# A first feed-forward product of ternary numbers, with its rank part as a product of its own

## What is computed

```python
def _bitlinear(x, w_latent):
    scale = jnp.clip(jnp.mean(jnp.abs(w_latent), axis=1, keepdims=True), 1e-05, None)
    tern = jnp.clip(jnp.round(w_latent / scale), -1.0, 1.0)
    w = w_latent + (tern - w_latent)
    return x @ (w * scale).T
h = _bitlinear(x, w_fc) + gate * (x @ v.T @ fast_b.T @ u.T)     # 256 -> 1024, rank 16
r = jnp.maximum(h, 0.0)
x = layernorm(x + _bitlinear(r * r, w_proj))                    # 1024 -> 256
```

## Time and profile before

| | |
|---|---|
| median of 3 runs | 2974.2 us (2971.97 to 2974.21) |
| the profiled execution | 2975.85 us |
| its span | 2974.1 us |
| mean granted clock of TensorE | 0.989 |
| busy, TensorE / VectorE / ScalarE / GpSimd | 97% / 80% / 73% / 64% |
| DMA | 57.54 MB, 19 GB/s over the span |

### The profile page before, as it was taken

One profiled execution on the slowest core, in us unless ns is written; L12 is line 12 of the kernel. 1 busy time (PEld: TensorE's weight loads), 2 busy tenths in 40 slices (PEclk: granted clock), 3 DMA queues, 4 the chain that ended last, 5 costly groups with the idle time before them and its releaser, 6 DMA issues.

```text
span 2974.1 us, 60896 instructions
## 1 busy us (share of the span) xinstructions
PE 2875.0 (97%) x20655; PEld 2306.4 (78%) x20655; DVE 2368.3 (80%) x6879; ACT 2164.4 (73%) x5699; POOL 1892.6 (64%) x2484
## 2 busy tenths in 40 slices
PE   7999999999999999999999995999999999999996
PEld 5677777777777777777777774778888888888885
DVE  6878978888888888798798787777777777777775
ACT  5766766776776776676676673677888888888884
POOL 5866866766776776676676684245555555555455
PEclk9999999999999999999999998999999999999998
DMA  2000000000000000000000003000000000000000
GB/s 73 22 9 16 23 9 16 23 9 16 23 8 16 23 8 16 23 9 16 23 9 16 23 29 100 8 8 8 22 19 19 15 15 15 15 15 15 8 15 22
DMA packets 51234, 57.54 MB, mean 19 GB/s; under 512 B 3024, under 2 KB 48608, under 8 KB 50928
## 3 DMA queue, kind: packets, MB, share of 16 engines
q1 hardware_dynamic: 49776, 51.94, 5.4%
q10 hardware_dynamic: 1152, 1.70, 0.2%
HBM read 36.86 MB, written 16.78 MB: 18 GB/s over the span
## 4 chain that ended last, share of the span: by engine, by line
PE 78%; ACT 9%; DVE 5%; issue 4%; POOL 3%; ACTq 0%; DVEq 0%; POOLq 0%
PE pj L299 17%; PE qk L364 9%; PE sc L335 9%; PE v_up L1321 7%; PE qk L379 6%; PE tp L354 5%; PE k L1321 4%; PE sc L354 4%; PE out L1412 3%; PE q L1321 3%; PE down L1412 3%; PE qk L310 3%; ACT b_y L96 2%; PE qk L317 2%; ACT b_ring L1504 2%
## 5 line engine op out<-in xcount | busy, mean ns | idle before, releaser
L719 POOL TENSOR_SCALAR a_ex<-a_ex,a_rc 128x384 f32<-128x384 f32 (+1 forms) x1024 | 535.1, 533 | 376.8 <-DVE a_rc L601 376.8
L488 ACT ACTIVATE a_ex<-a_ex,a_nm 128x384 f32<-128x384 f32 (+1 forms) x1024 | 575.3, 565 | 37.0 <-DVE a_nm L594 27.7
L594 DVE CUSTOM_DVE_ANT_0 a_ex<-sc,a_mask,a_rn 128x384 f32<-128x384 f32 (+1 forms) x1024 | 531.7, 543 | 8.7 <-PE sc L335 8.6
L1853 POOL TENSOR_TENSOR b_alo<-b_ring,b_ahi 128x512 fp32r<-128x512 f32 x128 | 169.4, 1324 | 415.8 <-DVE b_ring L1676 377.1
L494 ACT ACTIVATE a_pt<-tp 128x256 f32<-128x256 f32 (+1 forms) x512 | 222.7, 435 | 289.9 <-PE tp L354 289.9
L703 POOL TENSOR_TENSOR a_qr<-a_ra,a_rb 128x256 f32<-128x256 f32 x512 | 370.1, 734 | 89.7 <-DVE a_rb L576 89.7
L335 PE MATMUL sc<-a_kT,a_qT 64*64 64x256 f32 (+1 forms) x4096 | 307.6, 415 | 0.9 <-DVE a_nm L594 0.9
L364 PE MATMUL qk<-a_pt,a_v 128*64 128x384 f32 (+1 forms) x2048 | 303.9, 439 | 0.6 <-DVE a_pt L606 0.6
L606 DVE COPY a_pt<-sc 128x384 f32<-128x384 f32 (+1 forms) x400 | 203.7, 509 | 91.5 <-PE sc L354 86.2
L364 PEld LDWEIGHTS qk<-a_pt,a_v 128*64 128x64 f32 x2048 | 136.0, 136 | 142.5 <-issue 122.3
L575 DVE TENSOR_TENSOR a_ra<-pj,s_a_rot 128x256 f32<-128x256 f32 x512 | 212.8, 416 | 33.8 <-ACT s_a_sq L473 31.3
(11 more groups left out here) (279 smaller groups left out, 9166.0 us busy)
## 6 DMA issues: line engine op xcount, KB each, us to landing
s_res<-x SPq DMA_DIRECT2D x16, 512.0 KB, 3.9
y<-s_res SPq DMA_DIRECT2D x16, 512.0 KB, 2.9
s_y<-y SPq DMA_DIRECT2D x16, 512.0 KB, 3.9
a_xin<-x SPq DMA_DIRECT2D x15, 512.0 KB, 5.0
out<-b_y SPq DMA_DIRECT2D x15, 512.0 KB, 2.9
a_xin<-wqkv SPq DMA_DIRECT2D x8, 256.0 KB, 3.0
a_raw<-wqkv SPq DMA_DIRECT2D x3, 384.0 KB, 8.5
a_raw<-wqkv ACTq DMA_DIRECT2D x3, 384.0 KB, 12.0
```

The costliest lines, as they stand in the source:

```text
L488: e.activation(ex[h][w][:, 0:width], ex[h][w][:, 0:width], ACT.Exp, bias=nm[:, w, h:h + 1], scale=-1.0, accum_out=rs[:, w, h:h + 1]).then_ ...
L594: e.tensor_tensor_reduce(out=ex[h][w][:, 0:width], in0=SC[w % 2][h][:, 0:width], in1=mem['mask'][:, off:off + width], scale=rn[:, par, 4 * ...
L719: e.tensor_scalar(row, row, 0.0, rc[:, w, h:h + 1], ALU.add, ALU.mult).then_inc(g['exn_pool'], 1)
```

## The change

The up product is now made of the bare ternary numbers, which need no low part; scale and rank part are handled elsewhere.

- `mem['f_t']` holds the transposed ternary numbers. `pe_up` multiplies them with y3hi and y3lo, four products, and adds a fifth: `u_st` times `xv`.
- `xv` is v times the rows: `pe_rank_rows`, new, four products into the bank k, once for each sequence at c = 0. Then `dve_rank_rows`, new, reads that bank twice. The 128 rows of contraction are four strips of 32, in each of which 16 rank rows lie: strip 0 holds the rounded result (the subtraction takes nothing off there), strip 1 its low part, strip 2 the product with v's low part, strip 3 again the first. `u_st` has the rounded gate · fast_b · u / scale in strips 0 to 2 and its low part in strip 3.
- The scale of each output is applied on reading: `act_relu` gets `scale=st[:, 4, c:c + 1]`, `dve_square` multiplies by the same column in place of the maximum with 0.
- At c = 0, `pe_down` is called before `pe_up`.
- Preparation: the difference, the sum, the scaling, `pe_fc_rank`, `dve_fc_rank`, `act_fc_high`, `dve_fc_low` and `dve_rank` are gone. `dve_rank_up` and `dve_rank_down` come in at (-1, 3) and (-1, 4), and `pe_rank` gets eight transposes that spread 1 / scale over all partitions. The loads of w_proj wait for the ternary numbers (`tern_dve`) and no more for the sum.

```diff
     def pe_rank(e):
         for k in range(2):
-            e.matmul(O[k][0:RANK, :], mem['fb'], mem['u_t'][:, k * 512:(k + 1) * 512], start=True,
+            e.matmul(O[k][:, :], mem['fb'], mem['u_t'][:, k * 512:(k + 1) * 512], start=True,
                 stop=True).then_inc(w['bu_pe'], 1)
...
+        for k in range(2):
+            for t in range(4):
+                last = e.transpose(D[k][:, t * P:(t + 1) * P],
+                    st[:, 5, 4 * k + t:4 * k + t + 1].to_broadcast([P, P]), ident[:, :])
+            last.then_inc(w['inv_pe'], 1)
...
+    def dve_rank_up(e):
+        for k in range(2):
...
+            e.tensor_copy(raw[:, k * 512:(k + 1) * 512], O[k][:, :]).then_inc(w['u_dve'], 1)
...
+            e.scalar_tensor_tensor(raw[:, k * 512:(k + 1) * 512], raw[:, k * 512:(k + 1) * 512],
+                mem['gate'][:, 0:1],
+                D[k][:, :], ALU.mult, ALU.mult).then_inc(w['u_dve'], 1)
...
+        e.tensor_copy(mem['u_st'][:, :], raw).then_inc(w['rank_dve'], 1)
...
+        e.tensor_tensor(low, raw[3 * RANK_STEP:P, :], low.bitcast(F32), ALU.subtract).then_inc(w['rank_dve'], 1)
...
+    def pe_rank_rows(e, s):
+        e.wait_ge(g['y3l_dve'], 2 * s + 2)
...
+        if inside(s + 2):
+            e.wait_ge(g['ku_dve'], HC * (s + 3))
+        else:
+            e.wait_ge(g['sq_dve'], FC * s)
+        parts = [(c, x) for c in range(DC) for x in y3_split(s)]
+        for k, (c, x) in enumerate(parts):
+            last = e.matmul(K_BANK[:, :], mem['v_st'][:, c, :], x[:, c, :], start=k == 0, stop=k == len(parts) - 1)
+        last.then_inc(g['xv_pe'], 1)
...
     def pe_up(e, s, c):
...
-        pe_split_product(e, up_bank(s, c), mem['fhi'], mem['flo'], *y3_split(s), c).then_inc(g['h_pe'], 1)
+        bank, parts = (up_bank(s, c), [(k, x) for k in range(DC) for x in y3_split(s)])
+        for n, (k, x) in enumerate(parts):
+            e.matmul(bank[:, :], mem['f_t'][:, k, c * P:(c + 1) * P], x[:, k, :], start=n == 0, stop=False)
+        if c == 0:
+            e.wait_ge(g['xk_dve'], s + 1)
+        e.matmul(bank[:, :], mem['u_st'][:, c * P:(c + 1) * P], mem['xv'][:, :], start=False,
+            stop=True).then_inc(g['h_pe'], 1)
...
+        if c == 0 and inside(b - 2):
+            pe_rank_rows(e, b - 2)
         if c == 0 and inside(b + 1):
             pe_y2(e, b + 1, 1)
+        if c == 0 and inside(down[0]):
+            pe_down(e, *down)
         if inside(b - 2):
             pe_up(e, b - 2, c)
...
-        if inside(down[0]):
+        if c and inside(down[0]):
             pe_down(e, *down)
...
-        e.activation(mem['r'], up_bank(s, c)[:, :], ACT.Relu).then_inc(g['r_act'], 1)
+        e.activation(mem['r'], up_bank(s, c)[:, :], ACT.Relu, scale=st[:, 4, c:c + 1]).then_inc(g['r_act'], 1)
...
+    def dve_rank_rows(e, s):
+        e.wait_ge(g['xv_pe'], s + 1)
+        e.tensor_scalar(mem['xv'][:, :], K_BANK[:, :], mem['low_rows'][:, 0:1], None,
+            ALU.mult).then_inc(g['xs_dve'],
+            1)
+        e.wait_ge(g['xs_dve'], s + 1)
+        e.tensor_tensor(mem['xv'][:, :], K_BANK[:, :], mem['xv'][:, :].bitcast(F32),
+            ALU.subtract).then_inc(g['xk_dve'],
+            1)
...
-        e.scalar_tensor_tensor(mem['sq'][c % 2], up_bank(s, c)[:, :], 0.0, mem['r'], ALU.max,
-            ALU.mult).then_inc(g['sq_dve'], 1)
+        e.scalar_tensor_tensor(mem['sq'][c % 2], up_bank(s, c)[:, :], st[:, 4, c:c + 1], mem['r'],
+            ALU.mult, ALU.mult).then_inc(g['sq_dve'], 1)
```

More of the change, by code:

```diff
@@ L1063, in dve_biases, with dve_scales @@
         e.wait_ge(w['ready_dve'], 2)
[L1065 to L1068, removed]
+    def dve_scales(e, count, n, scale):
+        link(e, e.tensor_scalar(scale, st[:, 0, 0:count], 1.0 / n, SCALE_FLOOR, ALU.mult, ALU.max))
+        e.tensor_scalar(st[:, 2, 0:count], scale, 0.5, None, ALU.mult)
+        link(e, e.tensor_scalar(st[:, 3, 0:count], scale, -0.5, None, ALU.mult))
     def dve_fc_scales(e):
@@ L1089, in dve_fc_tern @@
                 fc_less[h][:, c, :], ALU.is_gt, ALU.subtract)
[L1090 to L1106, removed]
@@ L1107, in dve_fc_scaled @@
         last.then_inc(w['tern_dve'], 1)
-    def dve_rank(e):
-        e.wait_ge(w['wq_pool'], 4)
+        e.wait_ge(w['tern_dve'], h + 1)
+    def dve_rank_up(e):
+        e.wait_ge(i['rank'], 16 * 4)
+        raw = mem['u_raw']
         for k in range(2):
             e.wait_ge(w['bu_pe'], k + 1)
[L1113 to L1131, removed]
+            e.wait_ge(w['inv_pe'], k + 1)
+            e.tensor_copy(raw[:, k * 512:(k + 1) * 512], O[k][:, :]).then_inc(w['u_dve'], 1)
@@ L1244, in act_fc_rows @@
         e.wait_ge(w['tr_pe'], n + 1)
-        e.activation(fc_t[t][:, h * 512:(h + 1) * 512], D[n % 2][:, :], ACT.Copy).then_inc(w['tr_act'], 1)
-    def act_fc_high(e, c):
-        for k in range(2):
-            e.wait_ge(w['lr_dve'], 2 * c + k + 1)
-            cols = slice(k * 512, (k + 1) * 512)
-            e.activation(mem['fhi'][:, c, cols], fc_t[c][:, cols], ACT.Copy).then_inc(w['fhi_act'], 1)
+        e.activation(mem['f_t'][:, t, h * 512:(h + 1) * 512], D[n % 2][:, :], ACT.Copy).then_inc(w['tr_act'], 1)
     def act_proj_rows(e, n):
@@ L1791, in dve_step @@
             dve_q(e, b, c)
+        if c == 0 and inside(b - 2):
+            dve_rank_rows(e, b - 2)
         if c == 0 and inside(b + 1):
@@ L1989, in layers_memory @@
     mem['wq_hi'], mem['wq_lo'] = (sb(k, [P, DC, HD], F32R) for k in ('wq_hi', 'wq_lo'))
-    mem['fhi'], mem['flo'] = (sb(k, [P, DC, HID], F32R) for k in ('fhi', 'flo'))
+    mem['f_t'], mem['u_st'] = (sb('f_t', [P, DC, HID], F32R), sb('u_st', [P, HID], F32R))
+    mem['v_st'], mem['xv'] = (sb('v_st', [P, DC, P], F32R), sb('xv', [P, S], F32R))
     mem['proj_t'] = sb('proj_t', [P, FC, DIM], F32R)
@@ L2097, in chunk_columns, with in_rank_places @@
     return np.ascontiguousarray(w.transpose(2, 0, 1, 3).reshape(P, 3 * DC, HD))
+def in_rank_places(w):
+    out = np.zeros((w.shape[0], P), np.float32)
+    for k in range(P // RANK_STEP):
+        out[:, k * RANK_STEP:k * RANK_STEP + RANK] = w
+    return out
 def chunk_bias(v):
```

87 lines of the change are left out of this document (42 added, 45 removed).

## The result

| | before | after |
|---|---|---|
| median of 15 runs each | 2974.2 us (2969.6 to 2976.6) | 2981.25 us (2976.3 to 2984.6) |
| the profiled execution | 2975.85 us | 2981.36 us |
| its span | 2974.1 us | 2979.6 us |
| mean granted clock of TensorE | 0.989 | 0.989 |

What follows compares the result with a forecast made beforehand. TensorE was taken to bound the steady sequences, busy 67.04 of 67.12 us. Steady sequences 9.1, preparation 7.0 and end 1.0 make 17 us off the median 2974.2: 2957 us, range 2948 to 2968.

Steps and rivals of the forecast that it cites:

- The price of a product: TensorE: 0.233 us for each product of 512 columns, read from the trace; a skill page's 131 ns was not used.
- a product taken off TensorE there shortens the kernel by its issue time: Steady sequences, b = 2 to 14: each product saved gives 0.233 us, as long as nothing else gets late.
- the scale operands: Relu at 0.67 instead of 0.60 us, square 0.75 instead of 0.69, followed through step c = 0 of a steady sequence.
- v waits for the square in most steps: Rival, chance 0.17: in steady steps relu and square get slower, the other engines set the pace; 4 + 4 less, 2966.
- rank rows and order: Step c = 0: four rank products, two VectorE operations, down before up; the next up product 0.93 us late, sequence 0.70 shorter.
- v's wait at c = 1: Steady sequences, step c = 1: v waits 0.25 us on TensorE for the square of c = 0.
- just covered: k of step c = 1: y2lo ends at about 2121.15, TensorE is there at 2121.19, so no wait.
- the steady part: Thirteen sequences, b = 2 to 14, each 0.70 us shorter: 9.1 us less, bounds 4 and 15.
- for b = 15 and 16 nothing, since TensorE waits there for others: End: no gain in these two; the whole end 1 us less, between 3 less and 1 more.
- Preparation: Weight preparation at b = -1 and b = 0: 7.0 us less in sum, between 3 and 11.
- the plain fp32 products: Preparation, b = 0: rank products gone; 1.5 of 3.0 us count for the first, 1.9 for the second.
- the roundings, multiplications and subtractions: Preparation, b = 0: four of each gone from ScalarE and VectorE, 5.8 us of work, 3.1 us counted, lower bound nothing.

Runs made afterwards that it cites:

- e4: The kernel before with five products in each up in place of six, nothing else changed: 2955.0 us, ratio 0.9935.
- e6: The changed kernel without the rank rows and with up ahead of down again at c = 0: 2959.6 us, ratio 0.9958.
- e5: The changed kernel with relu and square as before, without the scale operand: 2972.9 us, ratio 1.0001.
- the staircase: Steady-sequence periods from the kernel before to the changed one: 67.10 before, 65.79 (e4), 66.21 (e6), 66.86 (e3), 67.33 changed.
- e3: The changed kernel without the rank products, their two VectorE operations and the wait for xv: 2970.8 us, ratio 0.9990.
- e11: The changed kernel with rank rows moved and partly on ScalarE, up first up to b = 15, scale applied once as a square: 2964.3 us, ratio 0.9972.

## Why the prediction was wrong

**The price of a product held.** The pitch is 0.233 again, no row shows 131 ns; steps 2 to 5 are 0.22 to 0.25 shorter, as said.

**Failed: "a product taken off TensorE there shortens the kernel by its issue time".** I counted 7 x 0.233 for steps 1 to 7 and one more at c = 0. e4 shows that two of the eight, those of c = 7 and c = 0, buy nothing there: 0.55 a sequence, 7 us. TensorE's 67.04 of 67.12 us busy hid that it was already meeting the chain of the others: the gap of 0.24 in the earlier trace rows, which I had read as a gain to come, was its sign.

**Failed: the scale operands at nothing in the steady steps.** I priced them rightly (relu 0.67, square 0.75; measured 0.68 and 0.75) but let them count at c = 0 only, and left "v waits for the square in most steps" to a rival with 0.17. They cost 0.42 a sequence (e4 to e6), 0.53 in the changed kernel (e5). By its mechanism, that rival is the one that came, with 62 waits, but it too forecast a faster kernel, by 8 us.

**Right, by a sum of two errors: rank rows and order.** I had 1.16 us a sequence for them (1.86 less 0.70); the staircase gives 0.65 + 0.47 = 1.12. In detail, the two new operations took 0.74 and 0.69 (0.75 and 0.69 forecast), and v's wait at c = 1 came. But k of c = 1, "just covered", waited 0.34, because VectorE's query operation ended 1.79 us after the rank products began, not 1.38: it was pushed back by the lateness of c = 7. VectorE's k operation, too, starts 3.54 us behind the first k product of the step, before 3.12, and in e4, with a product less and no other change, already 3.47. That the sum of the term is nearly right is luck.

Together 0.93 us a sequence, from -0.70 to +0.23 (67.10 to 67.33). Over the steady part that is 11 us of the error, -9.1 to +1.7; its first sequence, b = 2, is still 0.65 shorter than before (67.62 to 66.97).

**Failed: the end, "for b = 15 and 16 nothing, since TensorE waits there for others".** What TensorE waits for there is itself behind the up product: in VectorE's queue the square stands ahead of the operation on the down product of the sequence before (b_psc), which GpSimd goes on with, and the query operation stands behind the statistics of GpSimd's sum (b_ln_bn). In the changed kernel at b = 15 (timelines of PE and VectorE):

```profile
2857.18 0.50 PE L1426 MATMUL v_up<-b_xv,b_u_st 128*128 128x512 f32 x1 [0.36 <-DVE b_xv L1680]
...
2865.63 0.50 PE L1286 MATMUL q<-b_y2hi,b_wq_hi 128*128 128x512 f32 x1 [3.02 <-DVE b_ring L1671]
```

```profile
2858.43 0.75 DVE L1689 SCALAR_TENSOR_TENSOR b_ring<-v_up,b_wst,b_ring 128x512 f32<-128x512 f32 x1 [1.31 <-ACT b_ring L1522]
2859.10 1.28 DVE L1717 TENSOR_TENSOR b_ring<-down,b_psc 128x512 f32<-128x512 f32 x2
2862.52 0.75 DVE L65 BATCH_NORM_STATS2 b_ln_bn<-b_y 128x6 f32<-128x256 f32 x2 [2.15 <-POOL b_y L1844]
...
2864.82 0.75 DVE L1671 SCALAR_TENSOR_TENSOR b_ring<-q,b_one_bq,b_ring 128x512 f32<-128x512 f32 x1
```

In the kernel before the same square starts 7.91 us behind the last k group, here 10.48. The wait of q that was 1.7 us at most is 3.0. Waits of PE from 2848 to the end, the first three:

```profile
PE down L1377 <- POOL b_rlo L1859: 10.3, 6, 3.5
PE q L1286 <- DVE b_ring L1671: 7.3, 4, 3.0
PE down L1377 <- DVE b_ring L1717: 3.3, 2, 1.7
```

The first two were 7.7 and 5.1. The part takes 125.97 us before, 123.4 in e4, 127.3 in e3 and e6, 131.65 after. So 4.3 us come in with the rank rows of the last three sequences, of the 7.1 that their products and VectorE operations take (3 x 0.93 and 3 x 1.43), and 24 products less, 5.6 us of TensorE, gave 2.5 (e4). Moving the rank rows, with up first at b = 15 and the scale applied once (e11), gave back 2.5. The 3.9 us between e4 and e6 have no shown cause: e5, without the scale operands, ends in 131.8 as the changed kernel does. These lengths are those of single executions whose granted clock in this part differs (0.93 before, 0.91 in e4, 0.88 in e6, 0.92 in e3, 0.94 after, 0.90 in e5), and how much of each difference is the clock's is not shown either.

**Preparation: too large.** -4.0 for -7.0, inside my bounds of 3 to 11. Up to the third step of b = 0 the gain is 2.5 us (3.9 forecast), in the rest 1.5 (3.1). No experiment takes it apart, but the other traces run the same preparation, the old one in 3 of the 14 and the new one in 11 (in three of these with one small operation more). Up to the third step of b = 0 it took 54.9 to 55.1 us with the old weights and 49.6 to 53.0 with the new ones, 3.3 less in the mean; in the rest 106.0 and 105.8 in the mean. So the plain fp32 products gone are there, and of the 3.1 us for the roundings, multiplications and subtractions gone, hardly anything can be seen. A single pair of traces tells little here: e3 and e6, whose code is the same up to this point, took 53.0 and 49.6 us, at a mean granted clock of 0.85 and 0.94.

**Not explained.** The medians differ by 7.0 us, the profiled executions by 5.5 (that of the kernel before is 1.6 above its median), of which 2.1 lie in the part that was not touched. By the three other parts the change costs 3.4; where the rest is I can't say.
